# Four semaphores in turn for the scatters of GpSimd, one transfer in flight on each, in a graph network on one core

## The reference

```python
edge_index = jnp.stack([src, dst])
x = _layernorm(x + _L0_gnn_ref(x, src, dst), axis=-1)                 # segment_sum(x[src], dst)
x = _layernorm(x + _L1_gnn_ref(x, edge_attr_32, eps, W1, b1, W2, b2, edge_index), axis=-1)
x = _layernorm(x + _L2_gnn_ref(x, src, dst, edge_weight, weight), axis=-1)
x = _layernorm(x + _L3_gnn_ref(x, edge_index, w_src, w_tgt, gate_bias), axis=-1)
```

## Time and profile before

| what | us |
| --- | --- |
| median of 3 runs | 8733.82 |
| lowest and highest of them | 8688.12, 8753.31 |
| the profiled execution | 8791.13 |
| its span | 8789.4 |
| GpSimd busy | 4177.4 |
| VectorE busy | 6653.1 |
| PE busy | 5779.8 |
| ACT busy | 3968.4 |

### The profile page before, as it was taken

How to read it: one execution, slowest core, us unless ns; L and a number is a source line. 1 busy time by engine, 2 the same in 40 slices (tenths; PEclk the granted TensorE clock), 3 DMA queues, 4 the chain that set the end, 5 groups by cost and what they waited for, 6 DMA issues and landing times. The chain is left out here.

```text
span 8789.4 us, 287838 instructions
## 1 busy us (share of the span) xinstructions
PE 5779.8 (66%) x120824; PEld 5429.7 (62%) x120824; DVE 6653.1 (76%) x8079; ACT 3968.4 (45%) x5752; POOL 4177.4 (48%) x3710
## 2 busy tenths in 40 slices
PE   5777777999946666423222223677777775999995
PEld 4666666888846555423222223677777775999995
DVE  8999998999778887523233234588888888999994
ACT  2333333555435555322122122499898992333331
POOL 4455666566666666666666664000000002666662
PEclk8888888999977888766666666677777777999996
DMA  7877115777557777533333333366666663666661
GB/s 122 134 115 109 33 24 151 188 190 189 144 161 198 201 201 195 149 90 105 83 94 100 83 96 89 110 211 209 206 212 201 209 209 117 201 202 202 202 202 56
DMA packets 1123505, 1317.84 MB, mean 150 GB/s; under 512 B 581317, under 2 KB 869253, under 8 KB 1122183
## 3 DMA queue, kind: packets, MB, share of 16 engines
q1 hardware_dynamic: 768861, 739.56, 31.5%
q10 hardware_dynamic: 250536, 508.89, 20.3%
q0 software_dynamic: 103168, 54.68, 2.7%
HBM read 902.26 MB, written 400.43 MB: 148 GB/s over the span
## 5 line engine op out<-in xcount | busy, mean ns | idle before, releaser
L660 POOL DMA_INDIRECT slot_table<-recs,idx_now x3224 | 3312.9, 1028 | 2018.2 <-DMA slot_table<-recs,idx_now 1141.3
L1532 PE MATMUL banks<-hot_d,msg 128*96 128x256 bf16 x10192 | 1534.6, 305 | 1708.2 <-DVE msg L1017 1611.5
L1532 PEld LDWEIGHTS banks<-hot_d,msg 128*96 128x96 bf16 x10192 | 1255.1, 136 | 1836.0 <-DVE msg L1017 1570.1
L676 POOL TENSOR_TENSOR msg_z<-left,msg_z 128x448 bf16<-128x448 f32 x364 | 815.2, 2240 | 2395.1 <-ACT msg_z L1374 2395.1
L940 DVE TENSOR_TENSOR hot_d<-lodl,banks 128x2560 bf16<-128x2560 bf16 (+1 forms) x884 | 1485.1, 1680 | 0.2
L1305 ACT CAST near_now<-hot_t 128x1792 fp8e4<-128x1792 bf16 x364 | 613.4, 1685 | 1843.9 <-issue 1046.8
L1017 DVE TENSOR_TENSOR msg<-left,msg 128x448 bf16<-128x448 f32 x364 | 227.2, 624 | 1354.9 <-ACT msg L1318 1353.7
L1341 ACT CAST far_now<-hot_td 128x3584 fp8e4<-128x3584 bf16 x364 | 1153.9, 3170 | 34.9 <-DVE hot_td L958 32.5
L1586 PE MATMUL banks<-x_win,hot_td 128*128 128x32 bf16 x30576 | 881.4, 182 | 235.8 <-issue 217.7
L1586 PEld LDWEIGHTS banks<-x_win,hot_td 128*128 128x128 bf16 x30576 | 833.8, 100 | 251.8 <-issue 238.1
L1274 ACT CAST msg<-banks 128x480 bf16<-128x480 f32 (+1 forms) x1040 | 522.2, 554 | 500.4 <-PE banks L1532 463.6
(11 more groups left out here) (187 smaller groups left out, 10071.5 us busy)
## 6 DMA issues: line engine op xcount, KB each, us to landing
lo_bc<-row_table ACTq DMA_DIRECT2D x364, 448.0 KB
dl_bc<-row_table SPq DMA_DIRECT2D x364, 448.0 KB, 4.6
target_marks<-far_now SPq DMA_DIRECT2D x364, 448.0 KB, 3.2
dl_bc<-target_marks SPq DMA_DIRECT2D x364, 448.0 KB, 4.2
lo_bc<-row_table ACTq DMA_DIRECT2D x468, 320.0 KB
slot_table<-zeros SPq DMA_DIRECT2D x52, 1617.0 KB, 12.6
rec_in<-slot_table ACTq DMA_DIRECT2D x364, 231.0 KB
source_marks<-near_now ACTq DMA_DIRECT2D x364, 224.0 KB
```

What stands on the lines that cost most here:

```text
L660: pool.indirect_dma_start(out=slot_dram[c.number], out_offset=bass.IndirectOffsetOnAxis(ap=idx_now[:, c.slot, g:g + 1], axis=0), in_=recs[ ...
L676: pool.tensor_tensor(msg3[:, blk.slot, :, 2 * D:3 * D], left3[:, blk.slot], msg3[:, blk.slot, :, D:2 * D], ALU.subtract).then_inc(msg_made ...
L1532: mm = t.matmul(banks[0:3 * D, 6 + blk.par, 0:WIN], rows[:, blk.slot, g, :], hot[:, blk.slot, g // 2, :, g % 2], start=(blk.b == 0 and g = ...
```

## The change

The scatters signal four semaphores in turn, `scattered[g % 4]`, whatever the chunk's buffer. Before each scatter GpSimd waits until the last scatter on the same semaphore has landed, so at most four are in flight, one on each. The wait after every eighth scatter is gone. `spent` is counted three scatters later, before scatters 19, 35 and 51, when columns up to 15, 31 and 47 have landed. SP and ACT, and GpSimd at the end, wait for all four semaphores where they waited for one.

```diff
-RUN = 8
+LANES = 4
...
-        scattered = [sem(f"scattered{s}") for s in (0, 1)]
+        scattered = [sem(f"scattered{k}") for k in range(LANES)]
...
+        def landed(k, chunks, more=0):
+
+            return 16 * (chunks * len(range(k, G, LANES)) + more)
+
+        def wait_scattered(eng, chunks):
+            for k in range(LANES):
+                eng.wait_ge(scattered[k], landed(k, chunks))
...
-                        sp.wait_ge(scattered[c.slot], 16 * G * c.turn)
+                        wait_scattered(sp, c.number - 1)
...
                 for g in range(G):
+                    lane = g % LANES
+                    if c.number or g >= LANES:
+                        pool.wait_ge(scattered[lane], landed(lane, c.number, g // LANES))
+                    if g - (LANES - 1) in (16, 32, 48):
+                        pool.sem_inc(spent, 1)
                     pool.indirect_dma_start(
                         out=slot_dram[c.number], out_offset=bass.IndirectOffsetOnAxis(ap=idx_now[:, c.slot, g:g + 1], axis=0),
-                        in_=recs[:, c.slot, g, :], in_offset=None).then_inc(scattered[c.slot], 16)
-                    if g % RUN == RUN - 1:
-                        pool.wait_ge(scattered[c.slot], 16 * (G * c.turn + g + 1))
-                    if g + 1 in (16, 32, 48):
-                        pool.sem_inc(spent, 1)
+                        in_=recs[:, c.slot, g, :], in_offset=None).then_inc(scattered[lane], 16)
...
-            for slot in (0, 1):
-                pool.wait_ge(scattered[slot], 16 * G * TURNS)
+            wait_scattered(pool, NCH)
...
-                        act.wait_ge(scattered[blk.par], 16 * G * blk.turn + 16 * G)
+                        wait_scattered(act, blk.chunk + 1)
```

## The result

The changed kernel takes 8142.81 us (median of 4 runs, 8133.75 to 8160.64) beside 8732.83 us for the kernel before (4 runs): a ratio of 0.9327, with a 95% interval of 0.9297 to 0.9357. In two later jobs the ratio was 0.9362 (0.9342 to 0.9382) and 0.9363 (0.9344 to 0.9382). The profiled execution took 8141.59 us. Where a ratio stands with an interval, it compares the faster executions of both kernels, so it can differ a little from the ratio of the medians. The profiled execution of the kernel before (8791.13 us) is not one of those four runs, of which the longest took 8753.31 us: the two traces lie 650 us apart, the medians of one job 590 us.

What follows compares the result with a forecast made beforehand. GpSimd's scatters were taken to bound the kernel up to 5442 us. A gain of 752 less losses of 55, 25 and 10, taken as 660 us, off the 8733.82 us median gave 8074 us, range 7980 to 8240.

Steps and rivals of the forecast that it cites:

- (2): Landing waits left after 880 us, at chunk starts (27 us) and in the tail (28 us): loss 55 us, bounds 20 and 200.
- (4): Zeroing of the slot tables, until 880 us: loss 10 us, bounds a gain of 60 and a loss of 70.
- (1): Landing waits on the scatter line after 880 us, 850.2 us over 320, become ordinary gaps: gain 752 us.
- (3): Edge sweep runs freely for longer, until about 3950 us, making scatters beside it longer: loss 25 us, bounds 10 and 60.
- (5): A wait instruction on every scatter, 3224 in place of 364: taken as nothing; without cover up to 1600 us.
- (6): Record loads released three scatters later, and SP's and ACT's waits on four semaphores: cost nothing.
- The last step: From 8131 us for the profiled execution to the median of the runs, 57 us less: 8074 us.
- the signs: Expected in the new profile: last scatter near 4780 us, gap 0.30 us, remaining landing waits nearly all before 880 us.
- A: Rival: all landing waits on the scatter line vanish, the zeroing's too; gain 1033 us, 7701 us; chance 0.04.
- B: Rival: each scatter's wait costs 0.1 us, so 322 us come back; 8396 us; chance 0.09.
- C: Rival: the whole path of a wait stands in each gap between scatters, 940 us net slower; 9674 us; chance 0.05.
- D: Rival: landings stay as late per wait, so time is only moved; gain within 80 us, 8734 us; chance 0.03.

Runs made afterwards that it cites:

- the second job: Later job on another, undisturbed chip: kernel before 8791.92 us, changed kernel 8229.34 us (0.9362), changed kernel with eight semaphores 7890.12 us (0.8969).
- the third job: Disturbed job on another chip: kernel before 9825 us; it with a wait after every sixteenth scatter 11157.72 us; changed kernel with ten semaphores 11298.0 us.
- the fourth job: Undisturbed job on another chip: kernel before 8786.7 us, changed kernel 8221.54 us, kernel before with a wait after every sixteenth scatter 8358.5 us.

## Why the prediction was right, step by step

The forecast was 8074 us with a range of 7980 to 8240; 8142.81 us was measured. The mechanism is shown: scatters bound the kernel up to the end of the edge sweep (in each comparison of runs the time moved with the last scatter: 640 and 650 us between the first two profiles, 342 and 339 us between four and eight semaphores), a landing costs only what exceeds the slack (eight semaphores take the waits after 880 us away), and a met wait is free. The sum of 660 us was too large: within one job the gain was 590, 563 and 565 us.

- The end of the scatters: forecast 4781, measured 4800.8 us. That it is so close is partly luck: terms (2) and (4) below are off by about 70 us each, in opposite directions. In the two later jobs, where (4) brought nearly nothing, the last scatter started at 4875.1 and 4867.7 us.
- (1) and (2), the waits after 880 us: forecast 55 us left. Measured 210.2 us over 279, of which 279 x 0.30 = 84 are ordinary gap, so 126 us. In the two later jobs it was 236.6 us over 290 and 239.2 over 285, so 150 and 154 us. That is inside the bounds of 20 to 200 but two to three times the value taken, and it is the term that was mis-sized in all three. Of its two parts the chunk starts took 40 to 45 us in the three traces (forecast 27) and the tail, the waits anywhere else, 86 to 109 us (forecast 28): I took the mean of the waits as the wait of every scatter, yet the longest single wait from 2640 to 3500 us is 2.9 us on top of the slack.
- (3), the longer free sweep: 25 us forecast, 20.9 us more on the scatters (32.0 and 17.8 in the later jobs). The place where the sweep catches up, 4000 to 4050 us, is near the forecast of 3950, but the working given does not lead there: 36.6 us a chunk from 2473 us and 86 us a chunk from 82 us meet at 4244 us. The recorded working gives no other steps to 3950. (86 us a chunk is not the scatters' pace from the start either: the six chunks of the zeroing stage took 120 us or more.)
- (4), the zeroing stage: forecast a loss of 10 us with bounds from a gain of 60 to a loss of 70. It gained in the first profile after: by 880 us 418 scatters had been issued instead of 380, and the seventh chunk began 62 us sooner (807.96 instead of 870.05 us). The rows below are every fourth scatter of the first profile after, inside such a stretch (start, length, idle time before it):

```profile
329.05 0.96 POOL L673 DMA_INDIRECT slot_table<-recs,idx_now  x1 [0.30 <-issue]
...
339.52 1.31 POOL L673 DMA_INDIRECT slot_table<-recs,idx_now  x1 [5.69 <-DMA slot_table<-recs,idx_now]
...
350.13 0.96 POOL L673 DMA_INDIRECT slot_table<-recs,idx_now  x1 [4.15 <-DMA slot_table<-recs,idx_now]
...
360.79 0.97 POOL L673 DMA_INDIRECT slot_table<-recs,idx_now  x1 [4.59 <-DMA slot_table<-recs,idx_now]
...
371.16 2.11 POOL L673 DMA_INDIRECT slot_table<-recs,idx_now  x1 [4.44 <-DMA slot_table<-recs,idx_now]
```

  Four scatters take 10.4 to 10.7 us here, where the forecast had 12.0 with the landing of 11 us from the earlier trace rows. The scatter at 339.52 starts 9.5 us after the end of the one four before it (329.05 + 0.96). The zeroing transfers landed sooner as well, 10.9 us from issue to landing in place of 12.6, by the DMA rows of the two pages. But that is not the work of having fewer scatters in flight: in the second job these transfers took 12.3 us with four semaphores and 12.4 with eight, and in the third job 10.5 with a wait after every eighth scatter and 10.6 with ten semaphores. In the second and the fourth job the changed kernel had issued 382 scatters by 880 us, so there the gain was next to nothing, and the forecast's reckoning (a loss of 10 us) was near.
- (5), the met wait: nothing, shown.
- (6), loads and other waits: nothing late was seen; the first scatters of a chunk follow the copies as before.
- The last step, from the profiled execution to the median. For the profiled execution the working gives 8131 us, and it took 8141.59. That agreement says little, because the two profiled executions differ in more than the kernel: the one of before (8791.13 us) lies above all four runs beside which the change was timed and close to the kernel before in the second and fourth job (8791.92 and 8786.7 us), and the one of after is among its four runs. The forecast of the median, 660 us off 8733.82, missed by 69 us. Where the sum is too large is best read from the second job, whose kernel before took 8792 us like the first profile: 602.8 us of landing waits go beside the earlier trace rows (538.5 are left), the gaps grow by 7.6 us and the scatters by 32.0, which leaves 563 us; the last scatter starts 565 us earlier, and the time fell by 563 us. Of the 97 us that are missing there, term (2) has 95.
- Two of the signs did not come as stated. The landing waits that are left were to lie nearly all before 880 us; 210.2 of 470.8 us lie after it. And a chunk was to take 81 to 85 us from 2640 us on; it took 89 until 4000 us and 83 from there.

Of the rivals, A falls with the 260.6 us of waits that the zeroing stage keeps, B and C with the met waits, and D with the 640 us by which the scatters end sooner.

The Trainium skill's fixed cost of about 2.0 us per DMA of this kind (DMA: Bandwidth & Descriptors, "Anatomy of one DMA — SWDGE (gpsimd) path") does not hold beside the zeroing: waits of up to 6.4 us remain there with four in flight, on top of the 4.3 us of slack. Where the queues are idle the trace does not speak against it: no wait is left from 880 to 1320 us, and in the kernel before the idle time for a landing was 2.0 us on average there.

## What to carry to other kernels

A wait for the last of a batch of transfers pays the whole landing time once a batch. Give each of the last k transfers a semaphore of its own and wait for the one k before: in this kernel that costs nothing as long as k - 1 issues last longer than a landing, so size k from the longest landing of the busiest stage, not from the mean. (Here that is some 11 us, nine issues, so ten semaphores; this was not measured undisturbed, and eight still left 110 us of waits in that stage.) Check what the engine's pauses were good for to others before taking them away, on more than one chip.

## What the runs showed that I had not expected

- In two of the jobs, on chips of their own, PE, VectorE and ACT all but stopped while GpSimd scattered, and went on when it paused (1.44 and 0.14 us from one matmul of L1450 to the next, with ten semaphores): 340 to 4435 matmuls in 900 us instead of 9110, at a DMA share of 0.12 to 0.25. Eight semaphores, the best version on an undisturbed chip (0.897 of the kernel before), were there 1.091 of it, ten 1.150, and a wait after every sixteenth 1.094 and 1.135. What this change itself does there is open.
- Twice as many scatters in flight make a landing at most about 0.3 us longer (0.19 and 0.04 us within one job, 3.55 to 3.89 us between two jobs, at the same places of a chunk).
- The zeroing of the tables delays the landings but hardly the issuing: eight semaphores did the same stage in 96 to 101 us a chunk, beside 129 to 133 us of the kernel before.
